# Layer 0's opening: the second q half's rope behind the first half's split, VectorE copying the first projections, and matmuls of ones on TensorE

## The chip, the core and the metric

The kernel runs on one NeuronCore of a Trainium2 chip. Its engines are TensorE (PE in the profile, PEld for its weight loads), VectorE (DVE), ScalarE (ACT), GpSimd (POOL) and SyncE (SP), which issues the transfers. The metric is the device time of one execution, in microseconds (us); lower is better.

## The reference, cut to what matters

The model is two transformer layers over x of 4 batches, 512 tokens and 256 features. The change touches only the beginning of layer 0's attention:

```python
q = rms_norm(jnp.dot(x, q_kernel))     # 16 heads of 16
k = rms_norm(jnp.dot(x, k_kernel))     # 4 heads of 16
v = jnp.dot(x, v_kernel)
q = q * qcos + rotate_half(q) * qsin   # the rope; k likewise
logits = einsum('btkgh,bskh->bkgts', q * scale, k)
probs = softmax(logits)
```

After it come the output projection, a layer norm, a mixture of 8 experts with a shared expert, layer 1's causal attention and its 4-bit feed-forward block.

## The kernel before, in words

Every engine has a program of its own, and semaphores tie them. The order is written out by hand as strings of step names: `A_START` is the opening of layer 0, and `A_FIRST` to `A_LAST` are the attentions of its four batches, into whose gaps other steps are filled. All engines walk the same list `a_steps`; each does the part of a step that is its own, in the order of the list, and skips steps that have none. A sign ahead of a name moves it to another batch: `+Q0` in the opening is `Q0` of batch 1.

The steps that the change and the prediction speak of:

- `X0 X1` transpose x of a batch: four 128x128 transposes each on TensorE (line 648), copied to `x_t` by ScalarE (line 981).
- `Q0` to `Q3` are the products of 128 tokens with the 384 columns of the q, k and v weights (two matmuls each, line 656). ScalarE squares the q and the k columns with a running sum (lines 953 and 954, the results themselves go to `rot` and are not used) and copies all columns to `qkv` (line 955). The sums land in `ss`.
- `rp0 rp1 rp2` are VectorE's rope of k, of the first and of the second half of q (lines 1207 to 1216). `rp0` first waits for all four `Q` and computes the reciprocal root of the mean square (lines 1196 to 1201).
- `V0` copies v to `v_aug` (line 1223).
- `T0 T1 T2` transpose k and the two q halves on TensorE (line 648). ScalarE rounds the result to bf16 (line 962), and VectorE forms the two remainders (lines 1232, 1235 and 1236), so that three bf16 parts stand for one f32 number. I call the work of ScalarE and VectorE on a `T` its split. SyncE stores the parts in DRAM six times over (line 520) and loads them as stacks of 96 rows: k and the first q half (line 535), which the first scores wait for, and later the second q half (line 540).
- `attS` and `attP` are scores (line 711, with ScalarE's Exp, line 970) and the product with v (line 725). `rw0` is the transpose of the router's weights.

Steps that TensorE hands to another engine share three PSUM banks (5 to 7) in turn: a step waits until the step three places before it has been read. Banks 0 to 3 belong to the scores and are empty during the opening. `s_ones` counts two memsets that VectorE does first, of `ones` and of `v_aug`. `s_const` counts the loads of the rope's tables and of a triangle (`upper`); VectorE waits for them before anything else (line 1183) and casts the identity and the triangle (lines 1185 and 1186).

In ScalarE's order, the squares and copies of `+Q0` to `+Q3` stand ahead of the first Exp, and the first of them waits until VectorE has finished all three splits of batch 0 (`parts_ready`).

Of the kernel before, what the change touches and what calls it, by code (L numbers as in the profile page):

```python
# [25 lines left out]
ALU = mybir.AluOpType  # L26
ACT = mybir.ActivationFunctionType
AX = mybir.AxisListType

P = 128  # L30
B = 4
S = 512
C = 256
NC_ = C // P
NT = S // P
# [4 lines left out]
QK0 = C + KV0 * HD  # L40
QKV0 = C + 2 * KV0 * HD
# [28 lines left out]

A_START = """X0 X1 Q0 Q1 Q2 Q3 rp0 rp1 +X0 +X1 V0 T0 rp2 T1 T2 +Q0 +Q1 +Q2 +Q3 +rp0 +rp1 +rp2"""
A_FIRST = """.rw0 | | | | | +T0 .F0 | >X0 | +T1 | +T2 | .F1 | >X1 | | | .F2 | | |"""
A_SECOND = """-F3 .V0 +Q0 | -P0 | -P1 +Q1 | +Q2 | +Q3 | .F0 +rp0 +rp1 +rp2 | -N0 -N1 | -R0 -Sg0 | -Sg1
-Sg2 -Sg3 | +T0 -Su0 .F1 | +T1 +T2 | -Su1 -Su2 | -Su3 | .F2 | -D0 | -D1 |"""
# [73 lines left out]
def post_ln_layers(nc, ins, out):  # L150
# [4 lines left out]
    with ExitStack() as ctx:  # L155
# [197 lines left out]
        def sem(name):  # L353
            return ctx.enter_context(nc.semaphore(name))
# [11 lines left out]
        s_ones = sem("ones_ready")  # L366
        unit_full = [sem(f"unit_full{i}") for i in range(UNITS)]
        unit_free = [sem(f"unit_free{i}") for i in range(UNITS)]
        rope_done = sem("rope_done")
        v_ready = sem("v_ready")  # L370
        part1 = sem("part1_ready")
# [89 lines left out]
        def filled(eng, step):  # L461

            if step[:2] == OPENING:
                eng.wait_ge(max_full[step[2] % WIDE], step[2] // WIDE + 1)
                return ps[:, step[2] % WIDE, :]
            u = unit_no[step]
            eng.wait_ge(unit_full[u % UNITS], u // UNITS + 1)  # L467
            return ps[:, 8 - UNITS + u % UNITS, :]

        def consumed(eng, step):  # L470

            if step[:2] == OPENING:
                eng.wait_ge(max_free[step[2] % WIDE], step[2] // WIDE + 1)
                return
            u = unit_no[step]
            eng.wait_ge(unit_free[u % UNITS], u // UNITS + 1)
# [165 lines left out]
        def _(pe):  # L642
# [32 lines left out]
            def xg_turn(j, half, n, i):  # L675
# [4 lines left out]
                    last = nc.tensor.transpose(ps[:, 4, cols(c)], xg[:, half, cols(c)], ident)  # L680
                last.then_inc(xgt_ps, 1)

            pe.wait_ge(s_ident, 16)
            for step in a_steps:
                n, b, i = step
                if n == "rw":
                    pe.wait_ge(s_small, 96)
                    transposes(step, [(E * c, n_rw[0:E, cols(c)], ident[0:E, 0:E], P) for c in range(2)])
# [253 lines left out]
        def _(act):  # L942
            copy = ACT.Copy
            for step in a_steps:
                n, b, i = step
                if n == "Q":
                    if i == 0 and b:

                        act.wait_ge(parts_ready, 3 * b)
                        act.wait_ge(v_ready, b)  # L950
                    src = filled(act, step)

                    nc.scalar.activation(rot[:, i, 0:C], src[:, 0:C], ACT.Square, accum_out=ss[:, 0, i:i + 1])
# [130 lines left out]
        def _(v):  # L1084
            done = [0]

            def link(ins_):

                done[0] += 1
                ins_.then_inc(dve, 1)  # L1090
                v.wait_ge(dve, done[0])

            def tick(ins_):
                done[0] += 1
                ins_.then_inc(dve, 1)
# [84 lines left out]
            nc.vector.memset(v_aug, 1.0).then_inc(s_ones, 1)  # L1180
            v.wait_ge(s_ones, 2)
            v.wait_ge(s_ident, 16)
            v.wait_ge(s_const, 48)

            tick(nc.vector.tensor_copy(identb, ident))
            link(nc.vector.tensor_scalar(negmask, upper, NEG, None, ALU.mult))
            for step in a_steps:
                n, b, i = step
                if n == "rw":
                    nc.vector.tensor_copy(rw_t, filled(v, step)[:, 0:2 * E].rearrange("p (c e) -> p c e", c=2))\  # L1190
                      .then_inc(free_of(step), 1)
                elif n == "rp":
                    if i == 0:
                        for t in range(NT):
                            consumed(v, ("Q", b, t))
                        tick(nc.vector.tensor_scalar(rs_a[:, 0:NT], ss[:, 0, :], 1.0 / C, RMS_EPS, ALU.mult, ALU.add))
                        tick(nc.vector.tensor_scalar(rs_a[:, NT:2 * NT], ss[:, 1, :], 1.0 / (KV0 * HD), RMS_EPS, ALU.mult, ALU.add))
                        settle()
                        rsqrt(rs_a, rs_q, rs_b)

                        link(nc.vector.tensor_scalar(rs_q[:, 0:NT], rs_q[:, 0:NT], 0.25, None, ALU.mult))
# [429 lines left out]
```

## Time and profile before

| what | before |
|---|---|
| median of 3 runs | 854.17 us (853.47 to 854.2) |
| span of the profiled execution | 851.4 us |
| mean granted TensorE clock | 0.970 |
| busy PE, DVE, ACT, POOL | 90%, 52%, 42%, 14% |

The span reaches from the first to the last instruction of the profiled execution; its own time beside that is not listed, so the 2.8 us between the span and the median are taken as what lies around the span. In the page's 40 slices of 21.3 us each, the busy tenths of TensorE begin with 5 and 5 and stay at 7 to 9 until the end, and ScalarE's begin with 3, 3, 8 and 9. Of the granted clock the first three slices have 9, 6 and 9; nearly all the others have 9, the highest digit.

How to read it: busy shares are means over stages with different limits, so the stage that the change touches, the first 60 us, is read on its own, by stretches, and then in order of time.

### The profile page before, as it was taken

The numbers are of one execution on the slowest core, as the hardware profiler recorded it, in microseconds if no ns is written. First come the engines' busy times: TensorE is split into PE (matmuls) and PEld (weight loads), VectorE is DVE, ScalarE is ACT, GpSimd is POOL, SyncE is SP. The second block draws the span as 40 slices with busy tenths as digits, with TensorE's granted clock in tenths as the row PEclk, the third lists the DMA queues.
The fourth block names the chain that finished last, engine by engine and source line by source line (L and its number), as shares of the span: only waits on it lengthen the run. The fifth ranks groups of instructions, "written<-read, shape, count | busy, mean of one in ns | idle before, by whom it ended". The sixth has DMA issues, their size and how long they took to land. (4 is left out here: it accounts for less than half of the span.)

```text
span 851.4 us, 11512 instructions
## 1 busy us (share of the span) xinstructions
PE 767.9 (90%) x3907; PEld 409.4 (48%) x3908; DVE 446.6 (52%) x1198; ACT 359.7 (42%) x565; POOL 115.4 (14%) x127
## 2 busy tenths in 40 slices
PE   5599999999999999999997879888998989989886
PEld 3222444444435556666665445434464445533675
DVE  2744554565435622222247676868765674662453
ACT  3389775685684012212223233444423442156030
POOL 0000000000000311111842411231011110022000
PEclk9699999999999999999999899989999999999999
DMA  7567207005107161111125870006300370000000
GB/s 217 148 204 223 93 26 209 27 25 149 38 26 247 43 198 46 43 45 46 32 84 169 251 201 2 1 27 187 110 1 3 106 216 1 2 1 26 14 12 26
DMA packets 51582, 75.01 MB, mean 88 GB/s; under 512 B 7607, under 2 KB 44763, under 8 KB 49227
## 3 DMA queue, kind: packets, MB, share of 16 engines
q1 hardware_dynamic: 49660, 69.26, 27.0%
q0 software_dynamic: 1872, 5.11, 2.2%
q8 instruction: 29, 0.48, 0.2%
q14 instruction: 21, 0.16, 0.1%
HBM read 46.57 MB, written 27.66 MB: 87 GB/s over the span
## 5 line engine op out<-in xcount | busy, mean ns | idle before, releaser
L656 PE MATMUL ps<-arena 128*128 128x256 f32 (+3 forms) x1084 | 326.7, 450 | 18.2 <-issue 2.9
L656 PEld LDWEIGHTS ps<-arena 128*128 128x128 f32 x1084 | 201.2, 195 | 106.6 <-issue 68.7
L970 ACT ACTIVATE arena<-ps 128x1024 f32<-128x1024 f32 x128 | 124.2, 1027 | 32.9 <-PE ps L711 32.6
L1067 ACT ACTIVATE arena<-ps 128x1024 f32<-128x1024 f32 (+3 forms) x128 | 82.9, 702 | 114.1 <-PE ps L903 114.0
L1450 DVE TENSOR_REDUCE arena<-ps 128x1 f32<-128x512 f32 (+3 forms) x176 | 100.4, 633 | 28.5 <-PE ps L881 27.6
L769 PE MATMUL ps<-arena 128*128 x184 | 86.5, 593 | 0.6 <-DVE arena L1177 0.6
L711 PE MATMUL ps<-arena 96*128 96x512 bf16 x256 | 71.4, 390 | 7.0 <-DMA arena<-q_stacks_dram 3.9
L1565 POOL TENSOR_SCALAR_AFFINE_SELECT arena<-arena 128x512 f32<-128x512 f32 x64 | 41.7, 652 | 253.3 <-ACT arena L1067 253.3
L725 PE MATMUL ps<-arena 128*32 128x512 f32 x512 | 69.6, 611 | 2.9 <-DVE arena L1223 2.7
L879 PE MATMUL ps<-arena 96*128 96x128 bf16 (+3 forms) x256 | 62.3, 303 | 9.6 <-DVE arena L1450 5.7
L648 PE MATMUL ps<-arena 128*128 128x128 f32 (+3 forms) x237 | 38.6, 302 | 23.3 <-DVE arena L1216 10.5
L998 ACT ACTIVATE arena<-ps 128x512 f32<-128x512 f32 x23 | 13.8, 598 | 108.4 <-PE ps L769 108.4
L711 PEld LDWEIGHTS ps<-arena 96*128 96x128 bf16 x256 | 17.8, 98 | 82.6 <-ACT arena L970 40.7
L903 PE MATMUL ps<-arena 98*128 98x512 bf16 (+3 forms) x256 | 48.1, 308 | 7.4 <-ACT arena L1067 3.9
L916 PE MATMUL ps<-arena 128*32 128x128 f32 (+3 forms) x512 | 49.2, 458 | 3.2 <-DVE arena L1461 2.5
L881 PE MATMUL ps<-arena 128*128 128x128 bf16 x256 | 48.2, 220 | 0.0
L648 PEld LDWEIGHTS ps<-arena 128*128 128x128 f32 (+3 forms) x237 | 30.4, 152 | 33.3 <-issue 11.6
L769 PEld LDWEIGHTS ps<-arena 128*128 128x128 f32 x184 | 33.2, 190 | 24.9 <-issue 23.8
L786 PE MATMUL ps<-arena 128*128 x184 | 43.6, 380 | 0.8 <-ACT arena L1004 0.8
L879 PEld LDWEIGHTS ps<-arena 96*128 96x128 bf16 x256 | 25.0, 98 | 36.9 <-DVE arena L1450 22.5
L903 PEld LDWEIGHTS ps<-arena 98*128 98x128 bf16 x256 | 18.2, 98 | 50.6 <-issue 31.9
L786 PEld LDWEIGHTS ps<-arena 128*128 128x128 f32 x184 | 34.9, 190 | 15.1 <-issue 11.5
(153 smaller groups left out, 678.4 us busy)
## 6 DMA issues: line engine op xcount, KB each, us to landing
arena<-stacks_dram SPq DMA_DIRECT2D x16, 768.0 KB, 5.9
arena<-in_gate_up_proj SPq DMA_DIRECT2D x8, 1024.0 KB, 9.3
arena<-q_stacks_dram SPq DMA_DIRECT2D x8, 768.0 KB, 5.8
stacks_dram<-arena SPq DMA_DIRECT2D x16, 384.0 KB, 3.3
arena<-in_down_proj SPq DMA_DIRECT2D x8, 512.0 KB, 8.7
stacks_dram<-arena SPq DMA_DIRECT2D x16, 256.0 KB, 3.3
q_stacks_dram<-arena SPq DMA_DIRECT2D x8, 384.0 KB, 4.1
yg_dram<-arena SPq DMA_DIRECT2D x23, 128.0 KB, 1.7
```

The costliest lines, as they stand in the source:

```text
L648: last = nc.tensor.transpose(dst[0:rows, col:col + n], src, idn)
L656: last = nc.tensor.matmul(dst[0:rows, lo:hi], a, w, start=(n == 0), stop=(n == len(pairs) - 1))
L711: last = nc.tensor.matmul(ps[:, g, :], k_stack[0:STACK, b % 2, hg, cols(kt)], q_stack[0:STACK, b % 2, 4 * hg + g, :], start=True, stop=True)
L725: last = nc.tensor.matmul(ps[32 * g:32 * g + 32, 4, :], v_aug[:, kt, hg, :], (probs0, probs1)[i % 2][:, g, :], start=(kt == 0), stop=(kt = ...
L769: last = nc.tensor.matmul(ps[:, 2 * half + up, :], xg_t[:, half, c, :], gu[:, e, c, FE * up:FE * (up + 1)], start=(c == 0), stop=(c == 1))
L786: last = nc.tensor.matmul(ps[:, 6 + half, 0:C], hh_t[:, half, f, :], dn[:, e, f, :], start=(f == 0), stop=(f == NF - 1))
L879: nc.tensor.matmul(dst[:, w * g:w * (g + 1)], cq_stack[0:STACK, b % 2, h0 + g, cols(qt)], ck_stack[0:STACK, b % 2, h0 + g, 0:w], start=Tru ...
L903: last = nc.tensor.matmul(ps[:, g, P * kt:S], ck_stack[0:STACK + 2, b % 2, h, cols(kt)], cq_stack[0:STACK + 2, b % 2, h, P * kt:S], start= ...
L916: last = nc.tensor.matmul(ps[32 * g:32 * g + 32, 4, P * kt:S], cv_aug[:, b % 2, kt, 4 * hg + g, :], cprobs[:, i % 2, g, P * kt:S], start=( ...
L970: nc.scalar.activation(probs[:, 2 * p:2 * p + 2, :], ps[:, 2 * p:2 * p + 2, :], ACT.Exp)\
L1067: nc.scalar.activation(cprobs[:, i % 2, 2 * p:2 * p + 2, P * kt:S], ps[:, 2 * p:2 * p + 2, P * kt:S], ACT.Exp).then_inc(exp_done[p], 1)
L1450: nc.vector.tensor_reduce(mneg[:, qt, h0:h0 + nh], filled(v, step)[:, 0:nh * w].rearrange("p (h n) -> p h n", n=w), AX.X, ALU.max, negate= ...
```

## The change

In the hand-written order `T1` moves ahead of `rp2`. For batch 0, VectorE copies the projections from PSUM to `qkv`, and ScalarE, which waits for that copy, squares from `qkv`; a new semaphore `squared` tells VectorE when the sums are there. TensorE multiplies ones with ones into PSUM bank 0 to 3: ahead of everything two rounds of four products of 32 rows each and then two products of 128 rows, eight more ahead of batch 0's `T0` and six ahead of `T2`. VectorE's wait for the rope's tables moves to `rp0` of batch 0, and the two casts to the router's step. What is computed stays the same.

```diff
-A_START = """X0 X1 Q0 Q1 Q2 Q3 rp0 rp1 +X0 +X1 V0 T0 rp2 T1 T2 +Q0 +Q1 +Q2 +Q3 +rp0 +rp1 +rp2"""
+A_START = """X0 X1 Q0 Q1 Q2 Q3 rp0 rp1 +X0 +X1 V0 T0 T1 rp2 T2 +Q0 +Q1 +Q2 +Q3 +rp0 +rp1 +rp2"""
...
+        squared = sem("first_squares_done")
...
+            def keep_clock(n):
+
+                for _ in range(n):
+                    nc.tensor.matmul(ps[:, 0, :], ones, ones.unsqueeze(1).to_broadcast([P, NT, P]), start=True, stop=True)
+
+            pe.wait_ge(s_ones, 1)
+            for _ in range(2):
+                for g in range(4):
+                    strip = ones[32 * g:32 * (g + 1), :]
+                    nc.tensor.matmul(ps[:, g, :], strip, strip.unsqueeze(1).to_broadcast([32, NT, P]), start=True, stop=True)
+            keep_clock(2)
             pe.wait_ge(s_ident, 16)
             for step in a_steps:
                 n, b, i = step
+                if step == ("T", 0, 0):
+                    keep_clock(8)
+                elif step == ("T", 0, 2):
+                    keep_clock(6)
...
+                    if b == 0:
+                        consumed(act, step)
+                        nc.scalar.activation(rot[:, i, 0:C], qkv[:, i, 0:C], ACT.Square, accum_out=ss[:, 0, i:i + 1])
+                        nc.scalar.activation(rot[:, i, C:QK0], qkv[:, i, C:QK0], ACT.Square, accum_out=ss[:, 1, i:i + 1])\
+                          .then_inc(squared, 1)
+                        continue
                     src = filled(act, step)
...
             v.wait_ge(s_ident, 16)
-            v.wait_ge(s_const, 48)
-
-            tick(nc.vector.tensor_copy(identb, ident))
-            link(nc.vector.tensor_scalar(negmask, upper, NEG, None, ALU.mult))
             for step in a_steps:
                 n, b, i = step
-                if n == "rw":
+                if n == "Q" and b == 0:
+                    nc.vector.tensor_copy(qkv[:, i, :], filled(v, step)[:, 0:QKV0]).then_inc(free_of(step), 1)
+                elif n == "rw":
+                    tick(nc.vector.tensor_copy(identb, ident))
+                    link(nc.vector.tensor_scalar(negmask, upper, NEG, None, ALU.mult))
...
                         for t in range(NT):
                             consumed(v, ("Q", b, t))
+                        if b == 0:
+                            v.wait_ge(squared, NT)
+                            v.wait_ge(s_const, 48)
```

## Rows read from the trace of the kernel before

**Rows 1.** Stretches: their length, busy time (instructions) by engine, granted clock, DMA.

```profile
8.00:10.00 2.00, 2.00 (x4) 1.09 (x4) 0.00 (x0) 0.00 (x0) 0.00 (x0) 1.00 0.73 138
...
19.00:19.50 0.50, 0.00 (x0) 0.00 (x0) 0.47 (x3) 0.00 (x0) 0.00 (x0) 0.69 0.00 0
...
32.50:33.00 0.50, 0.50 (x3) 0.29 (x2) 0.31 (x1) 0.16 (x1) 0.00 (x0) 0.65 1.03 348
...
46.00:47.00 1.00, 1.00 (x6) 0.21 (x3) 0.93 (x3) 0.00 (x0) 0.00 (x0) 0.75 0.96 238
```

**Rows 2.** Timeline (start, length, what, idle before), the opening to the last product.

```profile
0.89 0.17 DVE L1179 MEMSET arena<- 128x128 f32 x1 [0.89 <-PEq L1613]
...
4.98 1.94 PE L648 MATMUL ps<-arena 128*128 128x128 f32 x8 [4.98 <-DMA arena<-in_x]
...
7.66 6.76 PE L656 MATMUL ps<-arena 128*128 128x384 f32 x13 [0.74 <-issue]
...
9.07 0.34 PEld L656 LDWEIGHTS ps<-arena 128*128 128x128 f32 x1 [0.30 <-issue]
...
12.27 1.86 PEld L656 LDWEIGHTS ps<-arena 128*128 128x128 f32 x6 [0.30 <-issue]
...
15.22 1.04 PE L648 MATMUL ps<-arena 128*128 128x128 f32 x8
...
15.42 0.39 ACT L953 ACTIVATE arena<-ps 128x256 f32<-128x256 f32 x1 [0.23 <-PE ps L656]
...
16.36 1.09 ACT L981 ACTIVATE arena<-ps 128x512 f32<-128x512 f32 x2
```

**Rows 3.** Timeline of VectorE: root, ropes and splits.

```profile
16.62 0.17 DVE L1196 TENSOR_SCALAR arena<-arena 128x4 f32<-128x4 f32 x1 [9.06 <-ACT arena L955]
...
21.00 0.42 DVE L1207 TENSOR_TENSOR arena<-arena 128x256 f32<-128x256 f32 x1
...
24.19 0.68 DVE L1232 TENSOR_TENSOR arena<-ps,arena 64x512 f32<-64x512 f32 x1
...
25.96 0.41 DVE L1207 TENSOR_TENSOR arena<-arena 128x256 f32<-128x256 f32 x1
...
28.92 0.69 DVE L1232 TENSOR_TENSOR arena<-ps,arena 128x512 f32<-128x512 f32 x1
...
30.93 0.69 DVE L1232 TENSOR_TENSOR arena<-ps,arena 128x512 f32<-128x512 f32 x1
```

**Rows 4.** Timeline: T2's transposes, and ScalarE's first work on the next batch's products.

```profile
28.94 1.11 PE L648 MATMUL ps<-arena 128*128 128x128 f32 x4 [3.83 <-DVE arena L1216]
...
32.84 0.38 ACT L953 ACTIVATE arena<-ps 128x256 f32<-128x256 f32 x1 [2.09 <-DVE arena L1236]
```

**Rows 5.** Timeline of SyncE's issues: the stores of the first q half's parts.

```profile
30.82 1.59 SPq L520 DMA_DIRECT2D q_stacks_dram<-arena  x3
```

**Rows 6.** Timeline: first scores, first, fifth and ninth Exp, VectorE's next split.

```profile
40.57 1.89 PE L711 MATMUL ps<-arena 96*128 96x512 bf16 x4 [3.90 <-DMA arena<-q_stacks_dram]
...
41.64 1.94 ACT L970 ACTIVATE arena<-ps 128x1024 f32<-128x1024 f32 x2 [3.88 <-PE ps L711]
...
47.37 3.90 ACT L970 ACTIVATE arena<-ps 128x1024 f32<-128x1024 f32 x4 [1.64 <-PE ps L711]
...
51.90 1.94 ACT L970 ACTIVATE arena<-ps 128x1024 f32<-128x1024 f32 x2 [0.62 <-PE ps L711]
...
58.57 0.68 DVE L1232 TENSOR_TENSOR arena<-ps,arena 64x512 f32<-64x512 f32 x1 [10.17 <-ACT arena L962]
```

**Rows 7.** Nearest rows for prices: three of the timeline, one group of VectorE by shape.

```profile
44.91 1.83 PE L725 MATMUL ps<-arena 128*32 128x512 f32 x8
...
56.66 0.60 PE L648 MATMUL ps<-arena 128*64 128x128 f32 x4
...
598.97 3.60 PE L656 MATMUL ps<-arena 128*128 128x512 f32 x8
...
L1450 DVE TENSOR_REDUCE arena<-ps 128x1 f32<-128x384 f32 x64 | 31.7, 549 | 10.5 <-PE ps L881 10.1
```

## The prediction

> **What bounds the kernel now.** I read the page's busy tenths first (where is the opening thin, where does an engine fill up), then busy time and granted clock by stretch [rows 1], then the order of time in the opening [rows 2 to 5], then the start of the attention [rows 6]. All that the diff touches but two casts lies before the first Exp of layer 0, at 41.64 us [rows 6]. Behind it the order of every engine is written out by hand and not changed, so what the opening gives is handed on from step to step: ScalarE is the full engine in the first batch's attention, TensorE in the batches that follow, and the transfers that either waits for are issued by the same chain. A start earlier by a microsecond is therefore worth about one.
>
> The opening is one chain. X is transposed at 4.98 [rows 2]. The four products of x with the q, k, v weights follow from about 7.66 and end at 15.22, where the next transposes begin (I call this end E). ScalarE squares and copies the last from 15.42 [rows 2]. VectorE starts the root at 16.62, has k's rope done at 21.00 and then does that of the first q half, splits k from 24.19, does the rope of the second q half from 25.96, splits the first q half from 28.92 and the second from 30.93 [rows 3]. SyncE stores the split of the first half from 30.82 and loads it back [rows 5]; the scores wait for that load and begin at 40.57 [rows 6]. So the first half's split, which the scores need, stands behind a rope which they don't need yet.
>
> TensorE is slow in three places. One weight load of the products takes 0.34 with 0.30 idle ahead of it, a pitch of 0.64; from 12.27 on six take 1.86, a pitch of 0.31 [rows 2]. The granted clock is shown as 1.00 from 8 to 10 [rows 1], but the pitch has halved by 12.27, so I take the stretch before it as the 1.2 GHz level. Later the row itself shows it: 0.69 from 19.00 to 19.50 (a fall at 19.2, after the transposes that end at 16.26 [rows 2]), 0.65 from 32.50 to 33.00 (a rise at 32.85), 0.75 from 46 to 47 (a rise at 46.5) [rows 1].
>
> **The change, part by part.** All times are against E, 15.2 in the profiled execution.
>
> *The matmuls of ones ahead of X.* They start when the ones are written, 0.89 + 0.17, about 1.1 [rows 2]. Two rounds of four 32-row strips, then two full products of 512 columns. No row shows four row strips. The nearest are four products of 32 columns each, which run beside each other: eight records (two to a product) take 1.83 at the lower level [rows 7]; two rounds are 3.5. A full product of 512 columns costs two records of 0.43 at the upper level (eight in 3.60 [rows 7]), 0.86, and 1.72 at the lower. So the block is 3.5 + 3.4 = 6.9 at the lower level and half that at the upper. The other bound is strips one after another: 8 x 1.72 = 13.8. I take the concurrent value, by the nearer row, and keep the other as a rival. The Trainium skill ("TensorE: Matmul & The Clock Gate", Part 3, Measured speedup) gives 3.07x for four row strips of 512 columns; by it the strips would cost about 4.5, an estimate, and X would stand some 0.5 later than in my sum. No run here shows it yet.
>
> When does the clock rise? In the three rises shown it came 3.9 to 7.3 us after the work started: 12.3 against 4.98, 32.85 against 28.94, 46.5 against 40.57 [rows 1, 2, 4, 6]. The middle is 5.6, so at 6.7. By then 5.6 of the 6.9 are done, the rest takes 0.65, and X starts at 7.35 rather than 4.98. From there on all is at the upper level: eight transposes in 1.04 instead of 1.94 [rows 2], then ScalarE's two copies, 0.6 each (1.09 for two [rows 2]), so the products start 2.0 after X (2.68 before), and take 16 records x 0.32 = 5.15 (7.56 before). E = 7.35 + 2.0 + 5.15 = 14.5: **0.7 us earlier**. With the rise after 3.9 it is 13.65 (1.6 earlier), after 7.3 it is about 15.25 (nothing).
>
> *VectorE copies the first projections, ScalarE squares from the copy.* This puts one engine more behind the last product: 0.2 to start, a copy of 384 columns (a reduction of 384 columns from the same memory takes 0.549 [rows 7]), then two squares with their sums, about 0.7 (the pitch of 0.94 from 15.42 to 16.36 less the copy that leaves it [rows 2]; that they read the copy and not the product is shown by no row, and I leave 0.2 either way). The root starts at E + 1.62, before at E + 1.42 [rows 3]: a cost of 0.2. Queued behind ScalarE's new wait are the copies of the next X, which nobody needs for 10 us; behind VectorE's only the rope. The casts of the identity and the triangle, now in the router step, move to a stretch in which VectorE is idle for 10.17 us ahead of its next work [rows 6], hence nothing; without that cover they cost 0.45.
>
> *Eight products of ones before T0.* The next X is transposed from E to E + 1.05, then 8 x 0.86 = 6.9: TensorE is free for T0 at E + 7.95. T0's four transposes take 0.60 at the upper level [rows 7], ScalarE's copy 0.6 and 0.2 to start, so k's split can start at E + 9.4. VectorE reaches it 24.19 - 16.62 = 7.57 after the root starts, at E + 9.2 [rows 3]. So the ones cost 0.2 here; queued behind them are T0, T1, T2, the next products and the scores.
>
> *The order T0, T1, second rope, T2.* k's split ends 1.77 later at E + 11.2, the first half's 1.87 later at E + 13.05 [rows 3]. Its stores are issued then, before at 30.82, E + 15.6 [rows 5]: 2.5 earlier. With the same 9.75 us from there to the scores [rows 5, 6] they can begin at E + 22.8 and the first Exp at E + 23.4; the load now meets the second half's stores later than before, which can only shorten it. What is late next? The second rope takes 2.95, to E + 16.0. The six products of ones end at E + 14.9, hidden. T2's transposes and copy, before beside the other split, now stand open: 0.05 + 0.60 + 0.2 + 0.6, and its split starts at E + 17.5 and ends 1.88 later, E + 19.4 (before E + 17.6). ScalarE's work on the next batch's projections waits for this split (32.84 before [rows 4]) and stands ahead of the first Exp in ScalarE's order: four of 0.94 (15.42 to 16.36 of the first batch, [rows 2]), now all filled in time by TensorE at the upper level, end at E + 23.2. The first Exp follows at E + 23.3, the same as the load gives. Before it was at E + 26.44: **3.1 us earlier**. The next rope starts at nearly the same time as before and keeps at least 3 us of slack to its transposes.
>
> *The clock at the attention.* TensorE now pauses at most 1.3 us between E and the scores, so I expect the upper level there. Before, the fifth Exp began at 47.37, 5.73 after the first, with ScalarE idle for 1.64 ahead of it; at the upper level four Exps of 0.97 and a wait of 0.6 as at 51.90 make 4.4 [rows 6]. **1.4 us earlier**, between 1.2 and 1.85.
>
> Sum: 0.7 + 3.1 + 1.4 = 5.2 us. The profiled execution has a span of 851.4, and the median of the runs is 854.17, so 2.8 lie around the span, which I keep. Span 846.2, time **849.0**. Its own range, by the bounds of the three terms (0 to 1.6; 2.6 to 3.6, with the load that much slower or faster; 1.2 to 1.85): 847.1 to 850.4.
>
> **The rivals.** *No rise from the ones* (R1): the clock rises only some 4.6 us after the products start, as the first rise did. Then the block costs 6.9 in full, X starts at 8.0 and the products at 10.65 at the lower level, E = 18.2, 3.0 later: 854.17 - 4.5 + 3.0 = 852.7. For it: each of the three rises had products or scores of real data ahead of it, and half of the block is strips, of which no row shows any. Against: the rest are full f32 products like those ahead of the first rise.
>
> *Strips one after another* (R2, the other side). The block is 17.2 at the lower level. If the clock rises at 6.7, X starts at 12.5 and E is 19.65: 854.17 - 4.5 + 4.45 = 854.1, no change. If it rises only when the full products start (14.9), X starts at 16.6 and E is 23.8, 8.6 later: 858.3, slower. The point from which it decides is X's start at 12.6. For it: strips differ in rows, not in columns, and no row shows such; against, eight records in 1.83 for the column form.
>
> *Absorbed later* (R3): the start is earlier but part of it is lost, on the next batch's rope (which starts no earlier in absolute time) or on the clock around later pauses. At half the gain: 851.6. For it: two thirds of the gain stand on ScalarE and the next batch's chain of VectorE gains nothing; against: the 10.17 us of idle time [rows 6].
>
> **How the numbers follow.** Forecast 849.0: 0.62. R1 852.7: 0.12. R2: 0.14, of which 0.07 no change and 0.07 slower. R3 851.6: 0.12. The range reaches to R1 and R3 and leaves R2 out, and has a little below the forecast's own lower end, since a rise in the clock may come sooner than in the three shown: 846.8 to 853.2; that leaves some 2 in 10 outside. About 0.2%, 1.7 us, is what a measurement of this kernel can tell from no change. Faster is the forecast, R3 and a small part of R1: 0.78; within it the rest of R1 and half of R2: 0.14; slower 0.08.
>
> **What would show it.** X's transposes starting near 7.35 and taking about 1.0; product weight loads at a pitch of 0.32 from the first; the root 1.6 after the last product; T1's stores issued some 13 us after E (near 27.5 in the trace's time); the first Exp near 37.8, and the fifth 4.4 later; a granted clock of 1.00 from the opening into the attention. Wrong would be: X starting after 12 (strips in series), a pitch of 0.64 in the products (R1), T0's transposes ending long after VectorE has reached k's split, the first Exp waiting for ScalarE's projections much beyond E + 23.3, or a first Exp that is 4 us earlier in a span that isn't (R3).

## The result: slower by 0.4%, and the profile after

The changed kernel takes 858.59 us (median of 15 runs), the kernel before 854.20 beside it: ratio 1.0041, 95% interval 1.0022 to 1.0059. Forecast was 849.0, so both the size and the sign were wrong. The profiled execution of the changed kernel has a span of 855.5 us. Medians here and below leave out one run of e7 in a slower state (871.77 us at a mean clock of 0.936). Every run on record lies 1.7 to 1.9 us above its own span, so of the 2.8 between the profiled span before (851.4) and the median only about 1.7 lie around the span; the rest is that this execution was a fast one. The forecast's difference of 5.2 doesn't hang on it.

The opening came out nearly as forecast. Timeline of the changed kernel up to the attention (start, length, engine, line, what, idle time before it and its releaser):

```profile
1.11 3.80 PE L693 MATMUL ps<-arena 32*128 32x512 f32 x16 [1.11 <-DVE arena L1201]
...
4.84 2.88 PE L687 MATMUL ps<-arena 128*128 128x512 f32 x4
...
7.55 1.04 PE L649 MATMUL ps<-arena 128*128 128x128 f32 x8
...
9.38 5.40 PE L657 MATMUL ps<-arena 128*128 128x384 f32 x16 [0.79 <-ACT arena L1003]
...
14.61 1.04 PE L649 MATMUL ps<-arena 128*128 128x128 f32 x8
...
14.81 0.56 DVE L1208 COPY arena<-ps 128x384 f32<-128x384 f32 x1 [0.73 <-PE ps L657]
...
16.38 0.17 DVE L1221 TENSOR_SCALAR arena<-arena 128x4 f32<-128x4 f32 x1 [1.01 <-ACT arena L970]
...
25.94 0.69 DVE L1257 TENSOR_TENSOR arena<-ps,arena 128x512 f32<-128x512 f32 x1
...
27.88 1.95 SPq L521 DMA_DIRECT2D q_stacks_dram<-arena  x3
...
32.17 0.69 DVE L1257 TENSOR_TENSOR arena<-ps,arena 128x512 f32<-128x512 f32 x1 [1.50 <-ACT arena L984]
...
34.08 0.38 ACT L975 ACTIVATE arena<-ps 128x256 f32<-128x256 f32 x1 [2.00 <-DVE arena L1261]
...
37.81 1.04 PE L727 MATMUL ps<-arena 96*128 96x512 bf16 x4 [1.00 <-DMA arena<-q_stacks_dram]
...
38.45 3.77 ACT L992 ACTIVATE arena<-ps 128x1024 f32<-128x1024 f32 x4 [0.47 <-PE ps L727]
...
44.41 1.94 ACT L992 ACTIVATE arena<-ps 128x1024 f32<-128x1024 f32 x2 [2.18 <-PE ps L727]
```

The strips run beside each other (3.80), X starts at 7.55, the first products end at 14.61 (before 15.22 [rows 2]), the first half's stores are issued at 27.88 (before 30.82 [rows 5]), the first Exp starts at 38.45 (before 41.64 [rows 6]). The gain is handed on: layer 1's first Exp comes 3.52 us earlier than before. There it is lost. Timeline of ScalarE, that Exp before, and after:

```profile
508.74 1.02 ACT L1067 ACTIVATE arena<-ps 128x1024 f32<-128x1024 f32 x1 [2.22 <-PE ps L903]
```

```profile
505.22 1.02 ACT L1089 ACTIVATE arena<-ps 128x1024 f32<-128x1024 f32 x1 [2.22 <-PE ps L919]
```

From there to the end of the span it is 851.43 - 508.74 = 342.7 us before and 855.52 - 505.22 = 350.3 after: 7.6 more, in code that the change doesn't touch. I call this stretch "layer 1" below. Stretches of the two traces (length, busy time and instructions of PE, PEld, DVE, ACT, POOL, granted clock, DMA share, GB/s), first after, then before:

```profile
8.00:10.00 2.00, 1.21 (x8) 0.84 (x7) 0.00 (x0) 1.08 (x2) 0.00 (x0) 1.00 0.56 154
19.00:19.50 0.50, 0.50 (x3) 0.26 (x2) 0.47 (x3) 0.00 (x0) 0.00 (x0) 1.00 0.00 0
...
41.00:44.00 3.00, 3.00 (x13) 0.76 (x13) 2.83 (x7) 1.23 (x2) 0.00 (x0) 0.50 0.87 233
...
549.50:552.50 3.00, 3.00 (x19) 0.82 (x15) 2.80 (x7) 0.64 (x2) 0.00 (x0) 0.50 0.00 0
...
635.00:638.00 3.00, 3.00 (x8) 2.38 (x8) 0.42 (x1) 0.00 (x0) 0.00 (x0) 0.50 0.02 5
686.00:689.00 3.00, 3.00 (x4) 1.01 (x3) 2.66 (x17) 0.00 (x0) 0.00 (x0) 0.50 0.36 126
```

```profile
549.50:552.50 3.00, 2.75 (x23) 1.20 (x22) 3.00 (x6) 1.80 (x3) 0.63 (x1) 1.00 0.00 0
...
635.00:638.00 3.00, 1.67 (x8) 1.52 (x9) 2.04 (x5) 0.27 (x1) 0.64 (x1) 1.00 0.00 0
686.00:689.00 3.00, 3.00 (x11) 1.11 (x13) 2.62 (x19) 0.74 (x2) 0.00 (x0) 1.00 0.43 150
```

After, the clock is at the lower level (0.50, 1.2 GHz) in places where before it is at the upper. Between 500 and 846 us the records of the granted clock show it low for 30.7 us after and 17.1 before. Some of these places cost dearly; the same 16 products of layer 1, TensorE's timeline, before and after:

```profile
636.33 3.69 PE L656 MATMUL ps<-arena 128*128 128x256 f32 x16 [1.56 <-DVE arena L1450]
```

```profile
634.63 5.38 PE L657 MATMUL ps<-arena 128*128 128x256 f32 x16 [1.57 <-DVE arena L1475]
```

The pause ahead of them is the same (1.56 and 1.57), yet one is followed by a fall and the other not. So a list of pauses alone doesn't tell what happened.

### The profile page after: what moved, and what is told of

It reads as the page before. It is cut to its first block and busy times, and to the rows that moved or that the text cites. A ratio compares the mean times of both kernels' runs of the same rounds, so it can differ in the third digit from the quotient of the medians.

```text
span 855.5 us, 11609 instructions
## 1 busy us (share of the span) xinstructions
PE 786.1 (92%) x3955; PEld 415.6 (49%) x3956; DVE 448.6 (52%) x1202; ACT 357.6 (42%) x561; POOL 116.0 (14%) x127
## 5 line engine op out<-in xcount | busy, mean ns | idle before, releaser
L992 ACT ACTIVATE arena<-ps 128x1024 f32<-128x1024 f32 x128 | 123.9, 1027 | 31.2 <-PE ps L727 30.7
L1020 ACT ACTIVATE arena<-ps 128x512 f32<-128x512 f32 x23 | 13.7, 597 | 108.4 <-PE ps L785 108.4
L649 PE MATMUL ps<-arena 128*128 128x128 f32 (+3 forms) x237 | 36.4, 289 | 10.3 <-DVE arena L1154 3.7
L919 PEld LDWEIGHTS ps<-arena 98*128 98x128 bf16 x256 | 18.5, 99 | 53.0 <-issue 32.8
```

The source lines that it names most:

```text
L649: last = nc.tensor.transpose(dst[0:rows, col:col + n], src, idn)
L919: last = nc.tensor.matmul(ps[:, g, P * kt:S], ck_stack[0:STACK + 2, b % 2, h, cols(kt)], cq_stack[0:STACK + 2, b % 2, h, P * kt:S], start= ...
L992: nc.scalar.activation(probs[:, 2 * p:2 * p + 2, :], ps[:, 2 * p:2 * p + 2, :], ACT.Exp)\
```

## The experiments

Five theories were tried. **A**: the earlier start puts the pauses of layer 1 elsewhere against the changes of the clock. **B**: the ones change what the clock does later. **C**: a transfer or a wait later on has become longer. **D**: the ones ahead of X cost the time by themselves. **E**, which came last: the 96 further instructions in TensorE's program move its instruction fetches into layer 1's pauses.

All runs in one table. "Instructions" are TensorE's products and weight loads by the page, against the kernel before (3907 + 3908); the ratio is to runs of the kernel before on the same chip, and medians from different sets differ by chip as well; "first Exp" and "layer 1" are of the profiled execution; "low" is the time between 500 and 846 us at the lower clock.

| kernel | instructions | first Exp | layer 1 | low | median us | ratio (95%) |
|---|---|---|---|---|---|---|
| e1 before again | 0 | 42.90 | 342.4 | 17.1 | 853.10 | 0.9982 (0.9963 to 1.0000) |
| e2 order alone | 0 | 39.89 | 343.5 | 20.5 | 853.13 | 0.9978 (0.9959 to 0.9997) |
| e3 no ones | 0 | 40.72 | 342.4 | 17.1 | 853.47 | 0.9985 (0.9969 to 1.0000) |
| e5 ones ahead of X | +40 | 39.85 | 342.9 | 17.1 | 851.34 | 0.9966 (0.9944 to 0.9989) |
| e6 ones ahead of T0, T2 | +56 | 39.64 | 342.9 | 17.2 | 850.15 | 0.9949 (0.9927 to 0.9971) |
| e14 the same | +56 | 38.94 | 342.8 | 17.5 | 850.05 | 0.9956 (0.9943 to 0.9970) |
| e9 five more | +66 | 39.35 | 342.7 | 18.5 | 849.06 | 0.9956 (0.9942 to 0.9970) |
| e10 ten more | +76 | 41.01 | 343.1 | 17.1 | 851.08 | 0.9972 (0.9960 to 0.9984) |
| after | +96 | 38.45 | 350.3 | 30.7 | 858.59 | 1.0041 (1.0022 to 1.0059) |
| e4 after again | +96 | 37.24 | 349.2 | 23.9 | 858.38 | 1.0042 (1.0022 to 1.0062) |
| e13 after again | +96 | 38.56 | 351.9 | 34.1 | 858.25 | 1.0055 (1.0040 to 1.0069) |
| e15 after, two copies | +96 | 38.18 | 349.3 | 30.7 | 861.77 | 1.0093 (1.0071 to 1.0115) |
| e16 after, four copies | +96 | 37.73 | 351.6 | 37.5 | 863.58 | 1.0102 (1.0085 to 1.0119) |
| e18 fast kernel, recut | +96 | 39.40 | 352.4 | 30.7 | 859.03 | 1.0057 (1.0036 to 1.0077) |
| e8 before, fill | +164 | 42.29 | 344.1 | 6.8 | 853.97 | 0.9983 (0.9963 to 1.0003) |
| e11 e6, fill | +220 | 38.56 | 345.9 | 13.7 | 847.47 | 0.9938 (0.9921 to 0.9954) |
| e17 after, recut | +256 | 37.94 | 343.4 | 24.2 | 849.82 | 0.9935 (0.9911 to 0.9959) |
| e7 after, fill | +260 | 38.13 | 343.1 | 7.6 | 847.81 | 0.9908 (0.9873 to 0.9943) |
| e12 the same | +260 | 37.19 | 343.1 | 9.1 | 849.64 | 0.9961 (0.9947 to 0.9976) |

**Parts of the change (e1 to e6).** e1 and e4 are copies of the two kernels. e2 is the kernel before with only the new order:

```diff
-A_START = """X0 X1 Q0 Q1 Q2 Q3 rp0 rp1 +X0 +X1 V0 T0 rp2 T1 T2 +Q0 +Q1 +Q2 +Q3 +rp0 +rp1 +rp2"""
+A_START = """X0 X1 Q0 Q1 Q2 Q3 rp0 rp1 +X0 +X1 V0 T0 T1 rp2 T2 +Q0 +Q1 +Q2 +Q3 +rp0 +rp1 +rp2"""
```

e3, e5 and e6 are the changed kernel without some blocks of ones (e3 without all, e5 without those ahead of T0 and T2, e6 without those ahead of X):

```diff
-            for _ in range(2):
-                for g in range(4):
-                    strip = ones[32 * g:32 * (g + 1), :]
-                    nc.tensor.matmul(ps[:, g, :], strip, strip.unsqueeze(1).to_broadcast([32, NT, P]), start=True, stop=True)
-            keep_clock(2)
...
-                if step == ("T", 0, 0):
-                    keep_clock(8)
-                elif step == ("T", 0, 2):
-                    keep_clock(6)
```

> The kernel before, unchanged, for its granted clock from execution to execution and a second trace. Theory A (the gain of the opening is real and is lost to low-clock stretches in layer 1 that come about by how its pauses of TensorE lie in time): the mean clock of its executions is nearly the same in all (spread under 0.004) and so are the times (853.4 to 856); behind 50 us the new trace has about the 27 us at the lower level that the first one has. Theory B (the products of ones bring the later low-clock stretches): the same here. Theory C (a fixed later cost, a transfer or a wait that the new order makes longer): the same here; low-clock time plays no part.

> The kernel before with T1 ahead of the second rope and nothing else. Both theories of the opening: the first q half's stores about 2.9 us earlier than 30.8, the first Exp 1 to 3 us earlier than 41.6, since T2's split ends later and the next products run partly at the lower level. Theory A: the time differs from the kernel before by the shift of the first Exps plus half of the change in low-clock time behind 50 us, within 1 us; low-clock time may well be above 27 us. Theory B: low-clock time behind 50 us stays at about 27 us, the time is 852 to 853. Theory C (the order makes a later wait longer): slower by 3 to 5 us as the full change, with pauses of TensorE behind 50 us that are longer than before.

> The full change without its products of ones (order, VectorE's copies and the moved casts stay). The first Exp about as with the order alone, within 0.5 us. Theory A: the time is again shift plus half of the change in low-clock time behind 50 us, which may be anything from 20 to 45 us. Theory B: without the ones low-clock time behind 50 us is back at 27 us, and the time is 852 to 853. Theory C: slower by 3 to 5 us.

> The full change, unchanged, for a second trace beside e1_before. Theory A: the first Exp is again near 38.4, the mean clock differs between executions by 0.006 or more and the time goes with it; the low-clock stretches behind 50 us lie at other pauses than in the first trace, or come in another number, while the pauses themselves keep their lengths. Theory B: low-clock stretches of the same total (41 us) in every execution. Theory C: low-clock time doesn't explain the times.

> The full change with the ones ahead of X only; those ahead of T0 and T2 are left out. Theory A, by now in a sharper form (without the later ones TensorE's clock falls between the first products and the next ones, and the rise that follows sets the first Exp, so everything behind lies the same way against the falls that come later): the first Exp lies about as far behind the last rise ahead of it as in the kernel before, the times stay together (clock of the executions within 0.005), 852 to 854, low-clock time behind 50 us 25 to 31 us. Theory B (ones bring later low-clock time): between the kernel before and the full change, low-clock time behind 50 us 30 to 35, 855 to 857.

> The full change with the ones ahead of T0 and T2 only; those ahead of X are left out. Theory A: the rise during the first products, as before at 12 us, sets E and all behind it, and there is no fall until layer 1. So the executions lie close together (clock within 0.005), but at a place of their own against the later falls: the time is first-Exp shift (2 to 4 us earlier) plus half the change in low-clock time behind 50 us, anywhere from 848 to 858, the same in all executions. Theory B: near the full change, 857 to 859, low-clock time behind 50 us about 38, with a spread of the clock as wide as the full change's 0.008.

Measured: 853.10, 853.13, 853.47, 858.38, 851.34, 850.15. No part alone is slower than before, with either block of ones alone the kernel is faster than before, both together make it slower by 4. The order and the copy give under 1.5 us without the ones (against e1, the copy of the kernel before, nothing). So the loss is no property of one part, and it doesn't add: in medians the block ahead of X gains 2.1 on e3, that ahead of T0 and T2 gains 3.3, both lose 4.9. The first of these gains isn't clear of noise (the intervals of e3 and e5 overlap).

**Warm pauses (e7, e8, e11, e12).** Products of ones in some twenty pauses of layer 1, added to the changed kernel (e7, and again e12), to the kernel before (e8) and to e6 (e11); they read and write nothing that is used:

```diff
+            def fill(dst, times):
+                one = ones.bitcast(BF16)
+                for _ in range(times):
+                    nc.tensor.matmul(dst, one[:, 0:P], one.unsqueeze(1).to_broadcast([P, 2, 2 * P]), start=True, stop=True)
...
+            pauses = {("cX", 1, 0): 7, ("cQ", 0, 0): 2, ("cQ", 1, 0): 2, ("cQ", 2, 0): 2, ("cQ", 3, 0): 2,
...
+                elif step in pauses:
+                    fill(take(pe, step), pauses[step])
```

> The full change, and bf16 products of ones (512 columns, 0.22 us each) in the pauses of TensorE in layer 1: ahead of the waits of cX, cQ, cN, cH, cM, of the first scores of a batch, of the last batch's cP, and of two more. They do nothing for the result. Theory A: most falls in layer 1 are gone, low-clock time behind 50 us at most 17 us instead of 34 to 41, and the time is 847 to 852, with less spread than the full change's 8 us. Theory B (more ones bring more low-clock time): slower than 858. Theory C (a fixed later wait): 858 to 862, since the products only add work.

> The kernel before with the same products of ones in the pauses of layer 1 and nothing else of the change. Theory A: low-clock time behind 50 us at most 15 us instead of 25 to 27, time 847 to 851; the full change with the same filling is then 2 to 4 us faster than this one, which is the gain of the opening with the falls taken away. Theory B: slower than 855. Theory C: the full change with filling is 3 to 5 us slower than this one.

> The change without the ones ahead of X, with the products of ones in the pauses of layer 1 as in e7_after_fill. Theory A: with most falls away it matters little where the pauses lie, so the ones ahead of X show their own worth in the opening (first Exp 1.2 to 2.4 us earlier): this kernel is 1 to 2.5 us slower than the full change with filling, 849 to 851, though without filling it was 8 us faster than the full change. Theory D (the ones ahead of X cost 8 us wherever the falls are): faster than the full change with filling, 840 to 845.

> The full change with the products of ones in the pauses of layer 1, once more beside e11_later_fill on the same chip. Theory A: 847 to 849.5, 1 to 2.5 us faster than e11_later_fill. Theory D: slower than e11_later_fill.

Measured: 847.81, 853.97, 847.47, 849.64. At first sight e7 shows that the clock's falls were the price. e8 speaks against that: its low time goes from 17.1 to 6.8 us and its layer 1 gets no shorter (344.1 for 342.7). e17 (below) has a layer 1 of 343.4 without any fill and with 24.2 us low, so filling isn't needed to mend the changed kernel. Whether it is what mended e7 stays open, since the fill changes the clock and the number of instructions at once. On one chip e12 is 2.2 slower than e11, where theory A had it faster; D had it slower, but put e11 at 840 to 845, and e17 speaks against D. By their ratios e7, e11 and e17 are the fastest kernels of the study, 0.6 to 0.9% below the kernel before (e12, which repeats e7, 0.4%); their intervals overlap those of e6, e9 and e14.

**Shifts of the start (e9, e10, e15, e16).** e9 and e10 put five and ten short products of ones ahead of the first scores in e6:

```diff
+                        if b == 0:
+                            one = ones.bitcast(BF16)
+                            for _ in range(5):
+                                nc.tensor.matmul(ps[:, 0, :], one[:, 0:P], one.unsqueeze(1).to_broadcast([P, 2, 2 * P]), start=True, stop=True)
```

e15 and e16 hold layer 1's first scores of the changed kernel back behind two and four idle copies on ScalarE, which add no instruction to TensorE's products; e13 and e14 are the changed kernel and e6 again, beside them:

```diff
+                    if b == 0 and i == 0:
+                        act.wait_ge(s_m, 32)
+                        for last in range(2):
...
+                            nc.scalar.activation(cprobs[:, 0, 0, :], ones.unsqueeze(1).to_broadcast([P, NT, P]), copy).then_inc(idled, 1)
```

> The change without the ones ahead of X (as e6_later_ones), and five bf16 products of ones, 1.1 us, ahead of the first scores, so that all behind the opening comes 1.1 us later against the rise of the first products. Theory A (what the falls of layer 1 cost goes by where its pauses lie against the times at which the clock can change): the executions stay close together, and the time from the first to the last Exps of layer 1's batches changes from e6's 94.2, 90.0 and 48.4 us; the time is 850.2 + 1.1 and another 1 to 6 us for this kernel or for e10_delay10. Theory D (the ones ahead of X bring the cost themselves, by whatever way, not by shifting what follows): 851.3 within 0.7 and the same three intervals.

> As e9_delay5 with ten products, 2.2 us. Theory A: the executions close together; 850.2 + 2.2 and another 1 to 6 us for this kernel or for e9_delay5, with intervals that differ from e6's in layer 1. Theory D: 852.4 within 0.7 and the intervals of e6.

> The full change, unchanged, beside e14_later_ones. Both theories: 856 to 860. Theory A: in the trace the first Exp of layer 1's second to fourth batches lies elsewhere against the times at which the clock can change than in e1, e2, e3, e5, e6, e9 and e10, where it is the same to 0.2 us for the fourth.

> The change without the ones ahead of X, unchanged, on the same chip as e13_after. Both theories: 849 to 852, 6 to 9 us faster than e13_after. If it is within 2 us of e13_after, the difference seen so far lay in the chips, and all comparisons between sets have to be dropped.

> The full change, and ahead of layer 1's first scores all engines of the attention idle for two copies of ScalarE of 128x512, about 1.3 us. They do nothing for the result. Theory A: layer 1 then starts where it does in the faster kernels (0.9 to 1.9 us into the raster of the clock's changes, 0.2 without the idling), and the kernel with 1.3 us of added idling is faster than the full change: 851 to 857. Theory D: the full change plus 1.3 us, 859 to 861.

> As e15_idle2 with four copies, about 2.5 us: layer 1 starts 2.7 us into the raster. Theory A: the time doesn't go with the idling; it differs from e15_idle2 by more than 1.2 us in either direction or lies below the full change. Theory D: the full change plus 2.5 us, 860 to 862.

Measured: 849.06, 851.08, 858.25, 850.05, 861.77, 863.58. Starts between 38.9 and 41.0 leave layer 1 of the fast kernel at 342.7 to 343.1, and two delays leave that of the changed kernel at 349.3 and 351.6. Neither theory had these times: e9 and e10 came out below both A and D, e15 above both, e16 above D (A gave it no time of its own), and why the idle copies cost 3.5 and 5.3 on e13 was not found. Nor do e9 and e10 test A: in their traces, as in those of all kernels with 0 to +76 and of e17, the clock falls 1.6 to 2.5 us after layer 1's first Exp, so the delay moved the start and the fall together. What speaks against A is that the clock falls at the same place in three traces of kernels with +96, e4, e13 and e18 (2.3, 2.1 and 1.9 us after that Exp), and that e15, which moves the fall to 0.4 ahead of it, is no faster. So where layer 1 starts against the clock doesn't separate the two groups. B and D fall as well with e5, e6 and e14: each block's ones are in a fast kernel (and both blocks in e17, below). C was left, without a reason why a transfer should be longer.

**Instruction fetches (e17, e18).** What does separate the groups is the column of instructions: all six kernels with +96 are slow, all others fast (the fills add most of theirs inside layer 1). The page of each kernel lists a queue "q8 instruction", 29 packets of together 0.48 MB before, about 16 KB each. In the trace of before 255 TensorE records lie between two of its packets on the average (27 intervals, from 186 to 327, without the one across the loop of the experts). So I take this to be TensorE's program being fetched, and 96 further instructions ahead of layer 1 move each fetch in it by more than a third of its period. In all six kernels with +96 a fetch starts between 3.6 and 0.8 us ahead of the first Exp of layer 1's second batch; in all nine with 0 to +76, and in e17, the nearest ones are 13 us or more ahead of it and 3 or more behind it. e17 keeps the whole change and cuts the blocks ahead of T0 and T2 into more, shorter products, so that TensorE has 256 instructions more than before; e18 takes e6 and recuts so that it has 96 more:

```diff
+            def keep_short(n, wide):
+                one = ones.bitcast(BF16)
+                for _ in range(n):
+                    if wide:
+                        nc.tensor.matmul(ps[:, 0, :], one[:, 0:P], one.unsqueeze(1).to_broadcast([P, 2, 2 * P]), start=True, stop=True)
+                    else:
+                        nc.tensor.matmul(ps[:, 0, 0:2 * P], one[:, 0:P], one, start=True, stop=True)
...
-                    keep_clock(8)
+                    keep_short(56, False)
...
-                    keep_clock(6)
+                    keep_short(52, False)
```

In e18 the two calls are keep_short(28, True) and keep_short(20, True).

> The whole change; only the products of ones ahead of T0 and T2 are cut differently: 56 and 52 bf16 products of 256 columns (about 6.4 and 6.0 us at the upper level, two instructions each) instead of 8 and 6 f32 products of 512 columns (6.9 and 5.2 us, four instructions each). The work and its time are about the same; TensorE has 160 instructions more than the changed kernel, so 256 more than the kernel before, exactly one 16 KB block of its instruction fetches. Theory E (the fetches that fall into layer 1's pauses cost the time): the fetches stand where the kernel before has them, the transfer of the max rows lands in 2.1 us and not 2.8 ahead of the second batch's scores, 848 to 852 us. Theory A (where the earlier start puts the pauses against the clock) and theory D (the ones ahead of X, by themselves): as the change, 856 to 860.

> The kernel with ones only ahead of T0 and T2 (850 us as e6 and e14), with these cut into 28 and 20 bf16 products of 512 columns (about 6.1 and 4.3 us, 96 instructions) instead of 8 and 6 f32 products (56 instructions). TensorE has then 96 instructions more than before, as many as the changed kernel, but nothing ahead of X. Theory E (the fetches of TensorE's instructions): they stand where the changed kernel has them, one in the pause ahead of layer 1's second batch, the max rows land in 2.7 to 2.8 us, 854 to 859 us. Theories A and D: as e6 and e14, 849 to 851.

Measured, both on one chip: e17 849.82, e18 859.03, the kernel before 854.33. Both are as theory E has it, which gives C its reason, and against A and D: the whole change is fast when the fetches stand where they stood before, and the kernel with a single block, no ones ahead of X, is slow when they stand where the changed kernel has them. Layer 1 is 343.4 in e17 and 352.4 in e18.

What the fetch meets is a small transfer. The scores of layer 1's second batch wait for the rows of the maxima, two transfers of 16 KB each. Transfers of the 8 us around it (queue: packets, MB, share; issues: KB, us to landing) and the first scores behind it, e14:

```profile
q1 hardware_dynamic: 64, 0.03, 1.7%
issues: line engine op xcount, KB each, median us to landing
arena<-arena SPq DMA_DIRECT2D x2, 16.0 KB, 2.1
...
557.24 1.04 PE L914 MATMUL ps<-arena 98*128 98x512 bf16 x4 [1.77 <-DMA arena<-arena]
```

and e18:

```profile
q8 instruction: 1, 0.02, 1.1%
issues: line engine op xcount, KB each, median us to landing
arena<-arena SPq DMA_DIRECT2D x2, 16.0 KB, 2.9
...
560.86 1.87 PE L923 MATMUL ps<-arena 98*128 98x512 bf16 x4 [3.31 <-DMA arena<-arena]
```

With the fetch beside it the transfer takes 2.9 instead of 2.1, TensorE's pause is 3.31 instead of 1.77, and the scores then run at the lower clock, 1.87 instead of 1.04. e17, with ones in both places and no fetch here, and e4, the changed kernel again:

```profile
556.98 1.04 PE L928 MATMUL ps<-arena 98*128 98x512 bf16 x4 [1.77 <-DMA arena<-arena]
```

```profile
556.25 1.25 PE L919 MATMUL ps<-arena 98*128 98x512 bf16 x4 [3.02 <-DMA arena<-arena]
```

A second place is shared by the traces of all six kernels with +96, and by none of the others. Some 28 us behind the second batch's first Exp, ScalarE waits until three stores of parts have landed in DRAM. Timeline before, and DMA from 584.1 to 588.2 (issues: KB, us to landing):

```profile
584.17 1.56 SPq L618 DMA_DIRECT2D stacks_dram<-arena  x3
...
588.17 1.27 ACT L1057 ACTIVATE arena<-ps,arena 128x512 f32<-128x512 f32 x2 [4.58 <-DMA stacks_dram<-arena]
...
stacks_dram<-arena SPq DMA_DIRECT2D x1, 128.0 KB, 3.0
```

and after, DMA from 579.4 to 585.0:

```profile
579.50 1.56 SPq L619 DMA_DIRECT2D stacks_dram<-arena  x3
...
584.96 1.27 ACT L1079 ACTIVATE arena<-ps,arena 128x512 f32<-128x512 f32 x2 [6.04 <-DMA stacks_dram<-arena]
...
q8 instruction: 1, 0.02, 1.0%
...
stacks_dram<-arena SPq DMA_DIRECT2D x1, 128.0 KB, 4.4
```

The last store lands in 4.4 instead of 3.0 (3.0 in e17 too). From the issue to ScalarE's work it is 5.46 to 5.50 in the six, each with a fetch that starts 2.6 to 3.2 ahead of that work; in the nine with 0 to +76, in e17 and with the fills it is 3.96 to 4.37.

**How far this is shown.** That the number of TensorE's instructions decides is shown by e17 and e18, in both directions. (Their blocks are also shorter in time than those that they replace, but in both alike, and the outcomes are opposite.) The first step, a fetch beside a transfer that an engine waits for, is in the rows: at the stores in all six traces with +96 (1.3 to 1.5 us), at the maxima in those of e4, e13, e15 and e18 (landing in 2.7, 2.8, 2.7, 2.9 us; in after and e16 in 2.1). What stays is the lower clock. The two groups of traces differ in where it falls against the second batch: 0.7 to 1.4 us after that batch's first Exp in the kernel before, in the eight others with 0 to +76 and in e17, from 1.1 before to 0.3 after it in the six with +96. In e4, e13 and e18 the late transfer makes this difference: the fall comes 53.1 to 53.5 us after layer 1's first Exp, as in the other group (52.8 to 53.7), but the batch comes 53.5 to 54.2 after it instead of 52.0 to 52.3. In the profiled execution of after no transfer was late there; the clock fell already at 549.4, 8 us ahead of that Exp, with no fetch near, and the scores come at the lower clock as well:

```profile
556.17 1.88 PE L919 MATMUL ps<-arena 98*128 98x512 bf16 x4 [1.75 <-DMA arena<-arena]
```

In e18 the way up to the second batch's first Exp takes 2.0 longer than in e14, of the 9.6 that its layer 1 is longer. With ScalarE's rows of both traces lined up, 6.2 of the other 7.6 come at four falls, three that e14 doesn't have (1.7, 1.7, 1.5) and one that is longer (1.3); the 16 products shown above lie at such a fall. How each of these later falls follows from the late transfers is not shown; I had no run that moves one fetch alone.

## Why the prediction was wrong, point by point

**Right: the ones ahead of X and the clock's rise.** Forecast was a block of 6.9 at the lower level, a rise at 6.7 and X at 7.35; X started at 7.55, took 1.04 and was followed by products of 5.40 for 16 records (forecast 5.15). E is 14.61 (14.5). The strips took 3.80 (3.5), which settles R2; one after another they would be 13.8 by the prediction's estimate. (Two readings of that sum are a little off: two rounds of 1.83 are 3.66, and eight records in 3.60 are 0.45 each and not 0.43.) That R2's slow case, 858.3, lies beside the measured 858.59 is an accident: its mechanism didn't happen. The Trainium skill ("TensorE: Matmul & The Clock Gate", Part 3, Measured speedup) has 3.07 times for four row strips; here it is 13.8 / 3.80 = 3.6 times, an estimate. R1 is settled by the lengths: X's eight transposes took 1.04 (1.94 before) and the products 5.40 for 16 records, 0.34 each. (The granted clock of 1.00 from 8 to 10 stands in the row of before too and can't settle it.)

**Right: VectorE's copies and the new order.** The copy takes 0.56 (0.549). The root starts at E + 1.77 (E + 1.62), T1's stores are issued at E + 13.27 (E + 13.05), ScalarE takes up the next products when T2's split is done at 34.08, and the scores wait last for the load ("1.00 <-DMA"), not for ScalarE. The first Exp is at E + 23.84 (E + 23.3).

**Half right: the clock at the attention.** The fifth Exp was to come 4.4 after the first. It did in e4 (37.24 to 41.69) and e14 (38.94 to 43.38). In the profiled execution of after it came 5.96 later, with a clock of 0.50 from 41 to 44, as it did in e17 (37.94 to 43.91). So this term of 1.4 (by its own rows 5.73 - 4 x 0.97 - 0.6 = 1.25) is there in some executions only; it is one that I should have given a chance and not a value. It doesn't explain the result, since e17 is fast without it.

**Right, and yet not enough: the opening is handed on.** Layer 1 starts 3.5 us earlier. With the fetches where they were (e17) the change gives 854.33 - 849.82 = 4.5 us, against a forecast of 5.2; by the interval of the ratio it is 3.5 to 7.6.

**Wrong: "behind it the order of every engine is written out by hand and not changed".** The step failed at the ones: I priced them by the time that they take (0.2 ahead of T0, hidden ahead of T2) and not by the 96 instructions that they add to TensorE's program. The order behind them is the same, its place in the fetched blocks is not, and so an opening earlier by 3.5 us was not worth 3.5. The missing term is 858.6 - 849.8 = 8.8 us (by the ratios of after and e17, 9.1), more than the whole gain. R3 named "the clock around later pauses", which is where the time went, but priced it as at most half of the gain, as if the worst were to lose what one had won. The rows to see it were in the profile of before: a line of the page for the instruction queue, which I took for overhead of the start. My rival for the slower side was looked for in the opening alone.

## What to carry to other kernels

Products or instructions that are put in for their effect on the clock lengthen a program, and all that follows is fetched at other moments: read the instruction queue in the windows of the pauses that matter, before and after. When two edits each gain and together lose, and the loss stands in code that neither touches, recut an edit to another number of instructions before looking for a cause in what it does. And compare stretches from one event to another (here layer 1's first Exp to the end: 342 to 346 against 349 to 352), which separated the two groups where the time at the lower clock didn't (e17 24.2, e4 23.9).

## What the hardware showed that I had not expected

A fetch of instructions, 16 KB in about 1 us and 0.2% of the DMA time by the page, isn't free where a short transfer stands beside it: landing went from 2.1 to 2.7 to 2.9 us in four profiled executions, and that of a store from 3.0 to 4.4. Kernels that differ in how many instructions stand ahead of layer 1, and so in the place of the fetches, differ by 9 us (e17 849.8, e18 859.0), 1%. The Trainium skill ("Runtime: NRT & Kernel Launch", Instruction fetch mechanics) states that each engine's instructions are refilled in 16 KiB blocks of 256 and that crossing a block is "mostly hidden". The 255 records between fetches agree with the first, and e17 was built on it; on the second the measurement differs, at least where TensorE or ScalarE waits for a transfer at that moment.

Time at the lower clock is a poor measure of loss. e17 spends 24.2 us of layer 1 there and e7 7.6, and their layers 1 take 343.4 and 343.1; e8 spends 10 us less there than the kernel before and takes 1.4 longer, though with products of its own to do. What cost here, beside the late transfers, were falls on a long run of products, as the 3.69 that became 5.38.
